# Node degrees by one-hot products: one-hot tables laid out with the tile number inside the class number

## The chip, the cores and the metric

The kernel runs on one core of a Trainium2 chip. The metric is the device time of one execution in microseconds (us). Five engines work side by side: PE (TensorE, matrix products; PEld is its weight load), DVE (VectorE), ACT (ScalarE), POOL (GpSimd) and SP (SyncE, which issues most plain transfers). They meet through semaphores.

## The reference, cut to what matters

A graph of 6250 nodes with 128 features and 106250 edges (each drawn edge in both directions, and a loop on each node) goes through two layers. The first is a graph convolution, the second an attention over edges. What the change touches is the number of edges that end in each node:

```python
deg = jax.ops.segment_sum(ones, dst, num_segments=n)
dinv = jnp.where(deg > 0, jax.lax.rsqrt(deg), 0.0)
norm = dinv[src] * dinv[dst]
msg = xw[src] * norm[:, None]
out = jax.ops.segment_sum(msg, dst, num_segments=n) + b
```

The kernel scales the normalised features of each node by `dinv` first, so no row of the first layer can be gathered before all degrees are known.

## The kernel before, in words

The edges lie as 832 tiles (`ET`) of 128: partition p of tile t holds one edge. The first block of the program does the following.

- **Degrees.** An end node `dst` is split in a low part (`dlo`, 0 to 63) and a high part (`dhi`, 0 to 97), both of 16-bit floats, `[128, 832]`. For each tile a one-hot table of 64 classes for the low part and one of 98 for the high part are made, and PE multiplies them: the product, 64x98, summed over all tiles in one PSUM bank, is the table of counts. The work goes in rounds of two slots, a slot holding 16 tiles (`BATCH`), 26 rounds in all (`ROUNDS`), 52 slots. `round` (line 340) makes DVE fill a slot with two comparisons, 1568 elements per partition for the high part (line 345) and 1024 for the low (line 346). PE takes the slot with 16 matmuls (line 794). With two slots DVE may fill one while PE reads the other: DVE waits on `hot_used` before it fills a slot again, PE waits on `hot_lanes`.
- **What lies between the rounds.** The first two calls of `round` stand before and in a loop of 13 iterations (line 350), each with one round and four `bn_stats` (line 355) on four tiles of the features `x`, which wait for the transfer of `x`. After the loop DVE does two reductions and a few small steps that wait for ACT and POOL (lines 358 to 366). Then 12 more rounds run with nothing between them (line 367).
- **The layout before.** A slot is `[16 tiles, classes]`, so a matmul reads 64 or 98 elements of 16 bits that lie one behind another. The comparison reads the row of class numbers `iota_h` again for each tile, and the tile's values from `dhi_twice` and `dlo_twice`, copies of `dhi` and `dlo` in which each value stands twice (lines 327 and 329), since the two comparisons run in inner pairs.
- **After the degrees.** One small step of DVE, two matmuls, a square root on ACT and a reciprocal give `dinv`. DVE scales all rows, `h`, in four parts (line 384), SP stores each to the table `y_tab` in HBM, and POOL waits for all four stores before its first gather (line 275). From there to the end of the block POOL issues 832 indirect gathers, one per tile of edges. A later block gathers rows of the second layer in 864 more.
- **ACT beside it.** It runs a warm-up, then counts by bucket (`sum_below`, line 680) from the moment when `buckets_ready` is given, which DVE does after the copies and four steps on `src`.

The order on each engine is as the code is written; no scheduler moves anything. All tables of one-hots and the `twice` copies lie in `sort_hi`, a buffer that is used for something else later on. `sort_v1` is idle during the whole degree stage.

Of the kernel before, what the change touches and what calls it, by code (L numbers as in the profile page):

```python
# [4 lines left out]
F32, F16, BF16 = mybir.dt.float32, mybir.dt.float16, mybir.dt.bfloat16  # L5
I32, U16 = mybir.dt.int32, mybir.dt.uint16
ALU = mybir.AluOpType
ACT = mybir.ActivationFunctionType
# [3 lines left out]
P = 128  # L12
# [13 lines left out]
ET = BODIES * BODY  # L26
EG = BODIES * GROUPS
LAST_TILE, LAST_FILL = EDGES // P, EDGES % P
HALF, HALVES = P // 2, 2 * NB
BATCH, SLOTS = 16, 2  # L30
# [27 lines left out]
def build(nc, x_in, src_in, dst_in, dst_rows_in, w0_in, b0_in, wqkv_in, bqkv_in, gamma_in, beta_in,  # L58
# [6 lines left out]
    def sem(name):  # L65
        return ctx.enter_context(nc.semaphore(name))
# [7 lines left out]
    with ctx:  # L74
# [58 lines left out]
        with ExitStack() as c1, nc.Block() as block:  # L133
            def sb1(name, shape, dt=F32):
                return c1.enter_context(nc.sbuf_tensor(name, shape, dt))

            def ps1(name, shape):
                return c1.enter_context(nc.psum_tensor(name, shape, F32))


            iota_h = sb1("iota_h", [P, 512], F16)
# [24 lines left out]
            dlo = sb1("dlo", [P, SORT_T], F16)  # L166
            dhi = sb1("dhi", [P, SORT_T], F16)
# [10 lines left out]
            tiles = sb1("tiles", [P, 2, NB])  # L178
# [11 lines left out]
            sort_v1 = sb1("sort_v1", [P, 2, SORTS, P], F16)  # L190
# [1 line left out]
            sort_hi = sb1("sort_hi", [P, 2, SORTS, max(WIDTH)], F16)  # L192

            flat_hi = sort_hi[:, :, :, :].rearrange("p a b c -> p (a b c)").bitcast(BF16)
            ohlo = flat_hi[:, 0:SLOTS * HALF * BATCH].rearrange("p (a b c) -> p a b c", a=SLOTS, b=BATCH)
            ohhi = flat_hi[:, SLOTS * HALF * BATCH:SLOTS * (HALF + HALVES) * BATCH].rearrange("p (a b c) -> p a b c", a=SLOTS, b=BATCH)
            twice_at = SLOTS * (HALF + HALVES) * BATCH
            dlo_twice, dhi_twice = (flat_hi[:, twice_at + n * 2 * ET:twice_at + (n + 1) * 2 * ET].bitcast(F16)
                                    .rearrange("p (t two) -> p t two", two=2) for n in range(2))
            tile_f, first_f = (flat_hi[:, n * 2 * SORT_T:(n + 1) * 2 * SORT_T].bitcast(F32) for n in range(2))  # L200
            b0_high = dhi[:, 0:2 * D].bitcast(BF16).rearrange("p (a b) -> p a b", a=2)
            b0_low = dlo[:, 0:4 * D].bitcast(F32).rearrange("p (a b) -> p a b", a=2)
# [4 lines left out]
            lane_i = tmp_i[:, 0:1]  # L207

            ps_sum = [ps1(f"ps_sum{k}", [P, 512]) for k in range(2)]
            ps_iota = ps1("ps_iota", [P, 512])  # L210
            ps_more = ps1("ps_more", [P, 512])
            ps_sort = [[ps1(f"ps_sort{n}{m}", [P, 512]) for m in range(2)] for n in range(2)]
            ps_row, ps_cnt, ps_deg = ps_sort[0][0], ps_sort[0][1], ps_sort[1][0]
            ps_run = ps_sort[1]

# [1 line left out]
            iota_ready, const_ready = sem("iota_ready"), sem("const_ready")  # L217
            ends_ready, rows_done = sem("ends_ready"), sem("rows_done")
            stats_done = sem("stats_done")
            shifted_ready, tiles_deg_done = sem("shifted_ready"), sem("tiles_deg_done")  # L220
            lanes_ready, deg_done = sem("lanes_ready"), sem("deg_done")
            hot_lanes, hot_used = sem("hot_lanes"), sem("hot_used")
            var_ready, std_done, norm_ready, h_done = sem("var_ready"), sem("std_done"), sem("norm_ready"), sem("h_done")
# [19 lines left out]
            def _(sp):  # L243
# [16 lines left out]
                sp.wait_ge(y_stored, 16 * Y_PARTS)  # L260


            in_twos = lambda t: t.rearrange("p k (c two) -> p k c two", two=2)
            every = lambda width: iota_h[:, 0:width].rearrange("p (c two) -> p c two", two=2)\
                .unsqueeze(1).to_broadcast([P, BATCH, width // 2, 2])
            each = lambda twice, tiles, width: twice[:, tiles, :].unsqueeze(2).to_broadcast([P, BATCH, width // 2, 2])

            @block.gpsimd
            def _(pool):
# [19 lines left out]
            def _(v):  # L289
# [34 lines left out]
                past = slice(LAST_TILE, LAST_TILE + 1)  # L324
                then(nc.vector.tensor_scalar(dlo[:, past], dlo[:, past], bad[:, :], None, ALU.add))
                nc.vector.memset(dlo[:, LAST_TILE + 1:ET], 2048.0).then_inc(lanes_ready, 1)
                nc.vector.tensor_copy(dhi_twice[:, :, :], dhi[:, 0:ET].unsqueeze(2).to_broadcast([P, ET, 2]))
                v.wait_ge(lanes_ready, 1)
                nc.vector.tensor_copy(dlo_twice[:, :, :], dlo[:, 0:ET].unsqueeze(2).to_broadcast([P, ET, 2])).then_inc(lanes_ready, 1)


                v.wait_ge(in_src, 16)
# [7 lines left out]
                def round(i):  # L340
                    for n in range(SLOTS):

                        v.wait_ge(hot_used, i * SLOTS + n + 1)
                        tiles = ds((i * SLOTS + n) * BATCH, BATCH)
                        nc.vector.tensor_tensor(in_twos(ohhi[:, n, :, :]), every(HALVES), each(dhi_twice, tiles, HALVES), ALU.is_equal)
                        nc.vector.tensor_tensor(in_twos(ohlo[:, n, :, :]), every(HALF), each(dlo_twice, tiles, HALF), ALU.is_equal).then_inc(hot_lanes, 1)

                v.wait_ge(lanes_ready, 2)
                round(0)
                with v.Fori(0, NODE_QUADS) as i:  # L350
                    round(i + 1)
                    v.wait_ge(in_x, 16)
                    part = ds(i * QUAD, QUAD)
                    for k in range(QUAD):
                        nc.vector.bn_stats(stats[:, part, :][:, k:k + 1, :], x[:, part, :][:, k:k + 1, :]).then_inc(stats_done, 1)
# [11 lines left out]
                with v.Fori(NODE_QUADS + 1, ROUNDS) as i:  # L367
                    round(i)
# [307 lines left out]
            def _(act):  # L676

                def sum_below(begin, end):

                    with act.Fori(begin, end) as i:  # L680
                        for n, unused in enumerate((tmp_f, away)):
                            b = i * 2 + n

                            act.wait_ge(below_ready, b + 1)
                            for part in range(2):
                                last = nc.scalar.activation(unused[:, PARTS[part]], sbk[:, PARTS[part]], ACT.Relu, bias=iota[:, ds(b + 1, 1)],
                                                            scale=-1.0, accum_out=below[:, part, ds(b + 2, 1)])
                            last.then_inc(below_ready, 1)
# [2 lines left out]
                act.wait_ge(const_ready, 1)  # L691

                nc.scalar.activation(warm[:, :], ones[:, 0:1], ACT.Sqrt)
                act.wait_ge(buckets_ready, 1)
                sum_below(0, EARLY)
                act.wait_ge(var_ready, 1)
# [3 lines left out]
                with act.Fori(0, NODE_QUADS) as n:  # L700
                    for k in range(QUAD):
                        j = n * QUAD + k
                        last = nc.scalar.activation(h[:, ds(j, 1), :], x[:, ds(j, 1), :], ACT.Relu, bias=nbias[:, ds(j, 1)],
                                                    scale=rstd[:, ds(j, 1)])
# [72 lines left out]
            def _(pe):  # L777
# [12 lines left out]
                with pe.Fori(0, ROUNDS) as i:  # L790
                    for n in range(SLOTS):
                        pe.wait_ge(hot_lanes, (i + 1) * SLOTS + n + 1)
                        for k in range(BATCH):
                            last = nc.tensor.matmul(ps_deg[0:HALF, 0:HALVES], ohlo[:, n, k, :], ohhi[:, n, k, :], start=False, stop=False)
                        last.then_inc(hot_used, 1)
                nc.tensor.matmul(ps_deg[0:HALF, 0:HALVES], zeros_h[:, 0:HALF], zeros_h[:, 0:HALVES], start=False, stop=True).then_inc(deg_done, 1)

# [2 lines left out]
                for n in range(2):  # L800
                    last = nc.tensor.matmul(ps_deg[:, HALVES:HALVES + NB], shifted[0:HALF, (1 - n) * HALF:(1 - n) * HALF + P],
                                            by_half[0:HALF, :].rearrange("p (j b) -> p j b", b=2)[:, :, n], start=n == 0, stop=n == 1)
# [3 lines left out]
                for n in range(2):  # L806
                    last = nc.tensor.matmul(ps_row[0:1, n * EG:(n + 1) * EG], ends_f[:, n:n + 1], ident[0:EG, 0:EG], start=True, stop=True)
# [42 lines left out]
                for part in range(2):  # L850
# [16 lines left out]
                    if part > 0:  # L867

                        pe.wait_ge(bk_ready, 2)
                        for g in range(ST // P):  # L870
                            c = g * P
                            last = nc.tensor.matmul(ps_sort[0][c // 512][0:1, c % 512:c % 512 + P], bk[:, 0, g:g + 1], ident[:, :],
                                                    start=True, stop=True)
# [3 lines left out]
                    for m in range(2):  # L877
                        last = nc.tensor.matmul(ps_sort[part][m][:, 0:w], zeros_h[:, 0:P], zeros_h[:, 0:w], start=False, stop=True)
# [4 lines left out]
        with ExitStack() as c3, nc.Block() as block:  # L883
            def sb3(name, shape, dt=F32):
                return c3.enter_context(nc.sbuf_tensor(name, shape, dt))
# [5 lines left out]
            a = sb3("a", [P, 2, QUAD, D])  # L891
# [674 lines left out]
```

## Time and profile before

| | us |
|---|---|
| median of 3 runs | 2404.34 |
| lowest and highest | 2402.21, 2406.58 |
| the profiled execution | 2402.21 |
| its span in the trace | 2400.4 |

```profile
PE 1599.1 (67%) x9620; PEld 1274.6 (53%) x9621; DVE 1776.6 (74%) x4811; ACT 1075.2 (45%) x3047; POOL 1683.3 (70%) x1772
```

The row gives the busy time of each engine in us, its share of the span and how many instructions it ran. No engine is busy all the time. Which one sets the pace changes from stage to stage, so the rows further down are taken by stage: start and duration of single instructions, what ended the idle time before them (in square brackets), and busy times in stretches.

### The profile page before, as it was taken

The page shows a single profiled execution, that of the slowest core. Times are in us where ns is not written, and L with a number is a line of the kernel's source. Part 1 is how long each engine was busy: PE and PEld are TensorE (multiplying, and loading weights), DVE is VectorE, ACT ScalarE, POOL GpSimd, SP SyncE. Part 2 cuts the span into 40 slices and gives each one's busy share as a digit, 9 for nine tenths or more (in the row PEclk, how much of TensorE's full clock was granted, in tenths as well). Part 3 has the DMA queues.
Part 4 walks back from the last instruction along what each step waited for, and adds up shares of the span by engine and source line. Part 5 has one row for each costly group of instructions (what it writes and reads, how often), then busy time and mean ns, then how long its engine had stood idle before and what let it go on. Part 6 is the DMA issues. An engine that isn't in the chain of part 4 may idle for free. (4 is left out here: it accounts for less than half of the span.)

```text
span 2400.4 us, 39858 instructions
## 1 busy us (share of the span) xinstructions
PE 1599.1 (67%) x9620; PEld 1274.6 (53%) x9621; DVE 1776.6 (74%) x4811; ACT 1075.2 (45%) x3047; POOL 1683.3 (70%) x1772
## 2 busy tenths in 40 slices
PE   5444439777878877777876665766766766676660
PEld 4334436555555555555655565655655655565560
DVE  9989999677767876667676666666666666666668
ACT  8734449777676877776751111111111111111113
POOL 0077777777777777777457777777777777777765
PEclk8857659888988888988989889789789788978875
DMA  2112211112121221121133333333333333333341
GB/s 89 54 51 53 53 52 52 52 51 52 52 52 52 53 52 52 52 52 52 26 127 104 104 104 104 104 105 105 104 104 104 105 104 102 103 105 104 104 98 54
DMA packets 84223, 186.36 MB, mean 78 GB/s; under 512 B 27773, under 2 KB 41213, under 8 KB 84069
## 3 DMA queue, kind: packets, MB, share of 16 engines
q0 software_dynamic: 68096, 167.88, 25.4%
q1 hardware_dynamic: 16101, 18.19, 2.3%
q8 instruction: 9, 0.15, 0.0%
q14 instruction: 17, 0.14, 0.0%
HBM read 173.11 MB, written 12.85 MB: 77 GB/s over the span
## 5 line engine op out<-in xcount | busy, mean ns | idle before, releaser
L1181 POOL DMA_INDIRECT kv_rows<-kv_tab,kv_idx x864 | 824.7, 955 | 274.5 <-issue 202.5
L283 POOL DMA_INDIRECT rows<-y_tab,idx x832 | 793.1, 953 | 308.6 <-issue 308.3
L1338 PE MATMUL ps_q<-q,hotT 128*128 x1744 | 312.5, 334 | 203.7 <-ACT hotT L1300 203.6
L763 ACT ACTIVATE sort_v<-sort_t,staged,minus 128x128 f16<-128x128 f16 x914 | 360.7, 480 | 114.8 <-PE ps_sort L860 113.1
L1338 PEld LDWEIGHTS ps_q<-q,hotT 128*128 128x128 f32 x1744 | 263.6, 231 | 257.9 <-issue 257.9
L602 DVE TENSOR_SCALAR sort_v<-iota_h,staged 128x128 f16<-128x128 f16 x748 | 250.7, 335 | 164.6 <-PE ps_sort L860 164.2
L860 PE MATMUL ps_sort<-sort_hi,sort_v 128*128 128x496 f16 x1662 | 366.2, 378 | 0.6 <-ACT sort_v L763 0.6
L818 PE MATMUL ps_sum<-rows,hot 128*128 128x128 f32 x1664 | 260.4, 322 | 145.3 <-DMA rows<-y_tab,idx 104.5
L1204 DVE TENSOR_TENSOR prod<-ps_q,kv_rows 128x512 f32<-128x512 f32 x216 | 149.4, 692 | 270.0 <-DMA kv_rows<-kv_tab,kv_idx 270.0
L1316 ACT ACTIVATE msg<-attc 128x32 f32<-128x32 f32 x216 | 49.5, 229 | 659.6 <-DVE attc L1216 659.6
L818 PEld LDWEIGHTS ps_sum<-rows,hot 128*128 128x128 f32 x1664 | 250.5, 237 | 159.8 <-issue 89.2
L1348 PE MATMUL ps_m<-msg,kv_hot 128*128 128x136 f32 x1728 | 306.8, 334 | 0.0
L755 ACT ACTIVATE sort_t<-iota_h,minus 128x128 f16<-128x128 f16 x831 | 250.9, 387 | 101.8 <-DVE minus L594 101.8
L1348 PEld LDWEIGHTS ps_m<-msg,kv_hot 128*128 128x128 f32 x1728 | 287.4, 244 | 0.0
L604 DVE TENSOR_SCALAR sort_hi<-iota_h,staged 128x496 f16<-128x496 f16 x831 | 286.1, 352 | 0.0
L1329 PE MATMUL ps_hT<-ident,kv_hot 128*128 128x128 f32 x876 | 157.7, 308 | 174.1 <-DVE kv_hot L1195 173.4
L1239 DVE TENSOR_TENSOR acc<-acc,ps_m 128x136 f32 x864 | 249.7, 289 | 21.9 <-PE ps_m L1348 20.3
L860 PEld LDWEIGHTS ps_sort<-sort_hi,sort_v 128*128 128x128 f16 x1662 | 165.5, 100 | 178.9 <-issue 11.3
L818 PE MATMUL ps_more<-rows,more_hot 128*128 128x128 f32 x768 | 143.0, 363 | 172.3 <-DMA rows<-y_tab,idx 105.3
L1300 ACT ACTIVATE hotT<-ps_hT 128x512 f32<-128x512 f32 x218 | 130.2, 597 | 236.6 <-PE ps_hT L1329 236.6
L818 PEld LDWEIGHTS ps_more<-rows,more_hot 128*128 128x128 f32 x768 | 133.2, 269 | 186.2 <-issue 185.7
L1329 PEld LDWEIGHTS ps_hT<-ident,kv_hot 128*128 128x128 f32 x876 | 111.1, 158 | 211.2 <-DVE kv_hot L1195 210.3
(236 smaller groups left out, 1864.1 us busy)
## 6 DMA issues: line engine op xcount, KB each, us to landing
kv_rows<-kv_tab,kv_idx POOLq DMA_INDIRECT x864, 2.7
rows<-y_tab,idx POOLq DMA_INDIRECT x832, 2.5
kv_tab<-kv SPq DMA_DIRECT2D x12, 512.0 KB, 2.9
x<-x_in SPq DMA_DIRECT2D x1, 3328.0 KB, 14.1
out<-h SPq DMA_DIRECT2D x12, 256.0 KB, 2.0
y_tab<-h SPq DMA_DIRECT2D x1, 1088.0 KB, 6.6
y_tab<-h SPq DMA_DIRECT2D x1, 960.0 KB, 5.7
y_tab<-h SPq DMA_DIRECT2D x1, 704.0 KB, 4.1
```

What stands on the lines that cost most here:

```text
L283: pool.indirect_dma_start(out=rows[:, k * SPAN + n, :], out_offset=None, in_=y_tab, in_offset=bass.IndirectOffsetOnAxis(ap=idx[:, k, n:n + ...
L602: nc.vector.tensor_scalar(sort_v2[:, k % 2, m, :], iota_h[:, 0:P], staged[:, LO, c:c + 1], staged[:, V2, c:c + 1], ALU.is_equal, ALU.mult)
L604: last = nc.vector.tensor_scalar(sort_hi[:, k % 2, m, 0:WIDTH[part]], iota_h[:, 0:WIDTH[part]], staged[:, HI, c:c + 1], None, ALU.is_equal)
L755: last = nc.scalar.activation(sort_t[:, k % 2, m, :], iota_h[:, 0:P], ACT.Abs, bias=minus[:, LO, k * SORTS + m:k * SORTS + m + 1])
L763: last = nc.scalar.activation(to[:, k % 2, m, :], sort_t[:, k % 2, m, :], ACT.Relu, bias=staged[:, v, c:c + 1], scale=minus[:, v, c:c + 1])
L818: last = nc.tensor.matmul(ps[:, 0:D], hots[:, n, :], rows[:, k * SPAN + n, :], start=n == 0, stop=n == SPAN - 1)
L860: last = nc.tensor.matmul(ps[:, 0:w], values[:, k % 2, m, :], sort_hi[:, k % 2, m, 0:w], start=False, stop=False)
L1181: pool.indirect_dma_start(out=rows[:, u, k, :], out_offset=None, in_=kv_tab, in_offset=bass.IndirectOffsetOnAxis(ap=idx[:, u, k:k + 1], ax ...
L1239: nc.vector.tensor_tensor(acc[:, ds(b, 1), :], acc[:, ds(b, 1), :], ps_m[u % 2][k // 2][:, k % 2:k % 2 + 1, 0:MSG], ALU.add).then_inc(tile ...
L1329: last = nc.tensor.transpose(ps_hT[u % 2][:, k, :], hot[:, u, k, :], ident[:, :])
L1338: last = nc.tensor.matmul(ps_q[u % 2][:, k, :], hotT[:, u % 2, k, :], q[:, ds(buckets[k], 1), :], start=True, stop=True)
L1348: last = nc.tensor.matmul(ps_m[u % 2][k // 2][:, k % 2, 0:MSG], hot[:, u, k, :], msg[:, u, k, :], start=True, stop=True)
```

## The change

The tables of a slot become `[classes, 16 tiles]`: the tile number runs fastest. The comparison now reads the values of 16 tiles straight from `dhi` and `dlo`, repeated for each class, and the class numbers from a new table `iota_b` in which each of 128 numbers stands 16 times. ACT makes it once, in `sort_v1`, between its warm-up and `sum_below`; DVE waits for it before the first round. The two `twice` copies go. PE reads a tile's table as every 16th element, a step of 32 bytes, for the weights (64 elements) and for the moving side (98). The bank of `ps_iota` moves from the third to the last place of the PSUM tensors, which shifts the banks of `ps_more` and `ps_sort` down by one.

```diff
-            ohlo = flat_hi[:, 0:SLOTS * HALF * BATCH].rearrange("p (a b c) -> p a b c", a=SLOTS, b=BATCH)
-            ohhi = flat_hi[:, SLOTS * HALF * BATCH:SLOTS * (HALF + HALVES) * BATCH].rearrange("p (a b c) -> p a b c", a=SLOTS, b=BATCH)
-            twice_at = SLOTS * (HALF + HALVES) * BATCH
-            dlo_twice, dhi_twice = (flat_hi[:, twice_at + n * 2 * ET:twice_at + (n + 1) * 2 * ET].bitcast(F16)
-                                    .rearrange("p (t two) -> p t two", two=2) for n in range(2))
+            ohlo = flat_hi[:, 0:SLOTS * HALF * BATCH].rearrange("p (a b c) -> p a b c", a=SLOTS, b=HALF)
+            ohhi = flat_hi[:, SLOTS * HALF * BATCH:SLOTS * (HALF + HALVES) * BATCH].rearrange("p (a b c) -> p a b c", a=SLOTS, b=HALVES)
+            iota_b = sort_v1[:, :, :, :].rearrange("p a b c -> p (a b c)")[:, 0:P * BATCH].rearrange("p (a b) -> p a b", a=P)
...
-            ps_iota = ps1("ps_iota", [P, 512])
             ps_more = ps1("ps_more", [P, 512])
             ps_sort = [[ps1(f"ps_sort{n}{m}", [P, 512]) for m in range(2)] for n in range(2)]
+            ps_iota = ps1("ps_iota", [P, 512])
...
-            in_twos = lambda t: t.rearrange("p k (c two) -> p k c two", two=2)
-            every = lambda width: iota_h[:, 0:width].rearrange("p (c two) -> p c two", two=2)\
-                .unsqueeze(1).to_broadcast([P, BATCH, width // 2, 2])
-            each = lambda twice, tiles, width: twice[:, tiles, :].unsqueeze(2).to_broadcast([P, BATCH, width // 2, 2])
+            every = lambda width: iota_b[:, 0:width, :]
+            each = lambda columns, tiles, width: columns[:, tiles].unsqueeze(1).to_broadcast([P, width, BATCH])
...
-                nc.vector.tensor_copy(dhi_twice[:, :, :], dhi[:, 0:ET].unsqueeze(2).to_broadcast([P, ET, 2]))
-                v.wait_ge(lanes_ready, 1)
-                nc.vector.tensor_copy(dlo_twice[:, :, :], dlo[:, 0:ET].unsqueeze(2).to_broadcast([P, ET, 2])).then_inc(lanes_ready, 1)
...
-                        nc.vector.tensor_tensor(in_twos(ohhi[:, n, :, :]), every(HALVES), each(dhi_twice, tiles, HALVES), ALU.is_equal)
-                        nc.vector.tensor_tensor(in_twos(ohlo[:, n, :, :]), every(HALF), each(dlo_twice, tiles, HALF), ALU.is_equal).then_inc(hot_lanes, 1)
-
-                v.wait_ge(lanes_ready, 2)
+                        nc.vector.tensor_tensor(ohhi[:, n, :, :], every(HALVES), each(dhi, tiles, HALVES), ALU.is_equal)
+                        nc.vector.tensor_tensor(ohlo[:, n, :, :], every(HALF), each(dlo, tiles, HALF), ALU.is_equal).then_inc(hot_lanes, 1)
+
+                v.wait_ge(lanes_ready, 1)
+                v.wait_ge(iota_b_ready, 1)
...
                 nc.scalar.activation(warm[:, :], ones[:, 0:1], ACT.Sqrt)
+                nc.scalar.activation(iota_b, iota_h[:, 0:P].unsqueeze(2).to_broadcast([P, P, BATCH]), ACT.Copy).then_inc(iota_b_ready, 1)
...
-                            last = nc.tensor.matmul(ps_deg[0:HALF, 0:HALVES], ohlo[:, n, k, :], ohhi[:, n, k, :], start=False, stop=False)
+                            last = nc.tensor.matmul(ps_deg[0:HALF, 0:HALVES], ohlo[:, n, :, k], ohhi[:, n, :, k], start=False, stop=False)
```

DVE before the change, from the last step on `dlo` to the first slot (all one-hot tables and both copies are parts of `sort_hi`):

```order
L326 MEMSET dlo 128x1 [waits dve]
L327 COPY sort_hi<-dhi 128x1664
L329 COPY sort_hi<-dlo 128x1664 [waits lanes_ready]
L333 MEMSET src_c 128x32 [waits in_src]
L334 TENSOR_SCALAR tmp_i<-src_c 128x832
L335 CAST sbk<-tmp_i 128x832 [waits dve]
L336 TENSOR_SCALAR sbk<-sbk,bad 128x1 [waits dve]
L337 MEMSET sbk 128x9 [waits dve]
L345 TENSOR_TENSOR sort_hi<-iota_h,sort_hi 128x1568 [waits hot_used,lanes_ready]
L346 TENSOR_TENSOR sort_hi<-iota_h,sort_hi 128x1024
```

The same place after the change (`sort_v` is the buffer that holds `iota_b`):

```order
L322 MEMSET dlo 128x1 [waits dve]
L326 MEMSET src_c 128x32 [waits in_src]
L327 TENSOR_SCALAR tmp_i<-src_c 128x832
L328 CAST sbk<-tmp_i 128x832 [waits dve]
L329 TENSOR_SCALAR sbk<-sbk,bad 128x1 [waits dve]
L330 MEMSET sbk 128x9 [waits dve]
L338 TENSOR_TENSOR sort_hi<-sort_v,dhi 128x1568 [waits hot_used,iota_b_ready,lanes_ready]
L339 TENSOR_TENSOR sort_hi<-sort_v,dlo 128x1024
```

The two copies are gone, everything behind them moves up, and the first comparison has one more thing to wait for. ACT at the start of the program after the change:

```order
L687 ACTIVATE warm<-ones 128x1 [waits const_ready]
L688 ACTIVATE sort_v<-iota_h 128x2048
L674 UNCONDITIONAL_BRANCH [waits buckets_ready]
L674 ISA
L680 ISA [waits below_ready]
L680 ACTIVATE cols,below<-sbk,iota 128x440
```

The step at line 688 is new; before, the wait on `buckets_ready` stood right behind the warm-up. PE's instructions are the same in number and order.

## Rows read from the trace of the kernel before

**Rows 1.** Stretches: start:end, us, POOL busy, granted PE clock, DMA share, GB/s.

```profile
121.00:1167.00 1046.00, 792.75 (x832) 0.83 0.20 52
1248.00:2335.00 1087.00, 824.15 (x864) 0.84 0.36 104
```

**Rows 2.** Waits of POOL: us in total, times, longest.

```profile
POOL rows L283 <- issue: 308.3, 831, 55.4
```

**Rows 3.** Timeline, 97 to 150: start, duration, instruction, idle before and releaser.

```profile
103.08 0.91 PE L794 MATMUL ps_sort<-sort_hi 128*64 128x98 bf16 x16 [0.58 <-DVE sort_hi L346]
...
105.12 0.21 ACT L708 ACTIVATE deg<-ps_sort 128x49 f32<-128x49 f32 x1 [8.12 <-PE ps_sort L801]
...
120.82 1.17 POOL L283 DMA_INDIRECT rows<-y_tab,idx  x1 [55.36 <-issue]
```

**Rows 4.** Timeline of DVE at the start of the degree stage.

```profile
7.16 1.02 DVE L327 COPY sort_hi<-dhi 128x1664 f16<-128x1664 f16 x1
...
9.07 0.09 DVE L333 MEMSET src_c<- 128x32 int32 x1
...
10.62 0.98 DVE L345 TENSOR_TENSOR sort_hi<-iota_h,sort_hi 128x1568 bf16<-128x1568 f16 x1
...
16.93 0.86 DVE L355 BATCH_NORM_STATS2 stats<-x  x4
```

**Rows 5.** Transfers: KB each, us from issue to landing; timeline of the issue of `x`.

```profile
x<-x_in SPq DMA_DIRECT2D x1, 3328.0 KB, 14.1
...
src_c<-src_in SPq DMA_DIRECT2D x1, 416.0 KB, 3.8
...
1.66 0.42 SPq L246 DMA_DIRECT2D x<-x_in  x1
```

**Rows 6.** Timeline of ACT: the warm-up, and a copy of 2560 elements per partition.

```profile
4.39 0.20 ACT L693 ACTIVATE warm<-ones 128x1 f32<-128x1 f32 x1 [2.31 <-DVE ident L315]
...
113.21 2.34 ACT L713 ACTIVATE acc<-h 128x2560 f32<-128x2560 f32 x1 [0.93 <-DVE h L384]
```

**Rows 7.** Timeline, second loop, at the high clock.

```profile
76.17 0.97 DVE L345 TENSOR_TENSOR sort_hi<-iota_h,sort_hi 128x1568 bf16<-128x1568 f16 x1
...
77.66 0.97 DVE L345 TENSOR_TENSOR sort_hi<-iota_h,sort_hi 128x1568 bf16<-128x1568 f16 x1
77.79 0.77 PEld L794 LDWEIGHTS ps_sort<-sort_hi 128*64 128x64 bf16 x16 [0.72 <-DVE sort_hi L346]
```

**Rows 8.** Timeline, second loop, at the low clock.

```profile
68.25 1.33 PEld L794 LDWEIGHTS ps_sort<-sort_hi 128*64 128x64 bf16 x16 [5.33 <-DVE sort_hi L346]
...
69.94 0.97 DVE L345 TENSOR_TENSOR sort_hi<-iota_h,sort_hi 128x1568 bf16<-128x1568 f16 x1 [0.25 <-PE ps_sort L794]
```

**Rows 9.** Timeline of DVE, first loop: the four `bn_stats` and the next slot.

```profile
28.16 0.87 DVE L355 BATCH_NORM_STATS2 stats<-x  x4
28.94 0.96 DVE L345 TENSOR_TENSOR sort_hi<-iota_h,sort_hi 128x1568 bf16<-128x1568 f16 x1
```

**Rows 10.** Stretches, line 794 alone: PE busy, PEld busy, granted clock, DMA share, GB/s.

```profile
26.00:42.00 16.00, 12.21 (x131) 10.79 (x132) 0.50 0.00 0
...
68.00:72.00 4.00, 3.43 (x38) 3.09 (x39) 0.50 0.00 0
74.00:103.00 29.00, 17.27 (x304) 14.62 (x304) 1.00 0.00 0
```

**Rows 11.** Timeline of DVE between the two loops.

```profile
62.65 1.22 DVE L358 TENSOR_REDUCE ends_i<-rows 104x1 int32<-104x1024 int32 x1
...
66.62 0.98 DVE L345 TENSOR_TENSOR sort_hi<-iota_h,sort_hi 128x1568 bf16<-128x1568 f16 x1
```

**Rows 12.** Timeline of PE: eight 32-bit matmuls of 128 columns, and that stretch's clock.

```profile
1300.21 1.15 PE L1338 MATMUL ps_q<-q,hotT 128*128 x8 [1.27 <-ACT hotT L1300]
1300.20:1301.40 1.20, 1.19 (x10) 1.19 (x11) 0.91 (x3) 0.00 (x0) 0.94 (x1) 1.00 0.36 109
```

**Rows 13.** Groups: a comparison with 32-bit operands; busy us, mean ns, idle before.

```profile
L450 DVE TENSOR_TENSOR hot<-ps_iota,rel 128x1024 f32<-128x1024 f32 x13 | 15.8, 1217 | 2.3 <-issue 2.3
```

More of the change, by code:

```diff
@@ L219, in build @@
             stats_done = sem("stats_done")
-            shifted_ready, tiles_deg_done = sem("shifted_ready"), sem("tiles_deg_done")
+            iota_b_ready, shifted_ready, tiles_deg_done = sem("iota_b_ready"), sem("shifted_ready"), sem("tiles_deg_done")
             lanes_ready, deg_done = sem("lanes_ready"), sem("deg_done")
```

## The prediction, made before the changed kernel ran

> **What bounds the kernel now.** I read the stages first. From 121 to 1167 us POOL issues the 832 gathers of the first layer and from 1248 to 2335 the 864 of the second [rows 1]: 792.75 us of busy time in 1046, which with a gap of 0.3 us before each gather is one gather per 1.25 us without a break. So everything behind the first gather is a fixed train, and it starts when the first gather may. The waits of POOL say how long that is: one idle time of 55.4 us stands before line 283, by far its longest [rows 2]. Then the timeline at that place [rows 3]: the last group of 16 degree matmuls starts at 103.08, ACT's square root at 105.12 had waited 8.12 us for PE, then DVE scales `h`, the stores follow, and POOL starts at 120.82. Nothing there has slack. The time of the kernel moves one for one with the end of the degree stage, and what the change does before about 104 us is the whole of its effect. All my sums are the shift of that end.
>
> Within the stage, DVE is the pace. At the high clock a slot costs it 77.66 - 76.17 = 1.49 us; PE starts a group 77.79 - 76.17 = 1.62 us after DVE began the slot, and feeds it in 0.77 us, 48 ns per matmul [rows 7]. PE has half its time left. At the low clock the group takes 1.33 us, 83 ns per matmul, which is one column per clock at 1.2 GHz (98 / 1.2 = 82 ns); and DVE got the slot back only 69.94 - 68.25 = 1.69 us after the group began, and had waited 0.25 us [rows 8]. So there the loop over two slots, 1.62 + 1.69 = 3.31 us, just exceeds DVE's own 2.98. That is the margin that this prediction turns on. In the first loop `bn_stats` adds 28.94 - 28.16 = 0.78 us [rows 9] and a round takes 3.76, more than 3.31.
>
> **The change part by part.**
>
> Copies. They go: from 7.16 to 9.07, 1.91 us off DVE [rows 4], and DVE begins the first slot at 8.71 instead of 10.62. `x` is issued at 1.66 and lands 14.1 us later, at 15.8; `src`, issued ahead of it, takes 3.8 and is there by 5.5, so it doesn't hold the step that moves up [rows 5]. The first `bn_stats`, at 16.93 before [rows 4], would come at 15.02 and wait 0.8 us for it. So the removal is worth 1.1 us where nothing else is late, and 1.9 where something else already is.
>
> `iota_b` on ACT. A copy of 2560 elements takes 2.34 us there [rows 6], so 2048 take about 1.9; it starts after the warm-up, at 4.6, and ends at 6.5, ahead of the 8.71 at which DVE wants it. Behind it on ACT stands `sum_below`, which waits for `buckets_ready` until 8.7 or later. Price 0; it would have to take twice as long before it cost anything. Its input repeats each element 16 times, which no row here shows; a price of nothing to 2 us more stays covered.
>
> The comparisons on DVE. Same element counts and types, all 16 bits wide with step 1 inside. A slot of 2592 elements in 1.49 us is 1.35 us at two elements per clock of 0.96 GHz and 0.14 of fixed cost. There is nothing to gain but the fixed part, 52 x 0.14 = 7 us at most; the far end is the comparison with 32-bit operands, 1.22 us for 1024 elements [rows 13], where the slot would take 3.1 us. Nothing in the new pattern speaks for either; price 0. The bank of `ps_iota`: 0, since the stage doesn't read it and no later wait hangs on DVE's comparisons.
>
> PE's reads. This is the disputed term. Number and order of the matmuls stay, but each column is now a separate 32-byte step, for weights and moving side. No row shows a 16-bit read of that kind. From below: 48 ns per matmul at the high clock, as now [rows 7]. From above: the 32-bit matmuls of the second layer, where PE takes in twice the bytes per column: eight of 128 columns in 1.15 us at a granted clock of 1.00 [rows 12]. Less the last one's 0.275 us (from there one end to the next) that is 125 ns each, 0.98 ns per column, or 96 ns for 98 columns. I take two clocks per column, 82 ns at 2.4 GHz and 163 at 1.2, near that row. The Trainium skill points the same way (SBUF — State Buffer, the note on cachelines under "Door 1: The DMA port swizzle"; also Advanced Engine Details and Errata, "SBUF Cachelines"): lines are 16 bytes, a reader needs about two hits on each to hide the memory's latency, and 16-bit data can be stepped by up to 8 elements for free. The step here is 16 elements. The pages give no size for the penalty; by their rule the sum is that of my forecast or of the slow rivals, and no run shown so far tests it.
>
> The sum with two clocks per column, clock levels as in the trace before (low until about 6 us after the first group, low again for about 4.5 us after the pause between the loops, high from 74 on [rows 10]):
> - copies: -1.9.
> - start, low clock: groups take 16 x 0.163 = 2.61 us. The first runs 10.33 to 12.94 and frees its slot 0.38 later, at 13.32; DVE was ready at 11.69: 1.63 late. The second ends at 15.55, frees at 15.93; DVE was ready at 14.81: 1.12 late. Less the 0.3 it waited before: +2.5. That also hides the wait for `x`.
> - rest of the first loop at the high clock: 1.62 + 1.69 = 3.31 is under 3.76: 0.
> - pause (62.65 to 66.62 [rows 11]): unchanged. After it again two low-clock groups, 1.63 + 0.74 late, less 0.3 that it waited before: +2.1.
> - eleven further rounds of the second loop: 3.31 against 2.98, 11 x 0.33 = +3.6.
> - last group, 1.31 against 0.77: +0.5.
> Sum +6.8 us on the profiled execution's 2402.2, which lies 2.1 under the median of 2404.3; against the median 2411. The form's own range: with less tail after a group about +5; with 0.98 ns per column a round of the second loop is 3.54 us and the sum near +10; and where PE stays at the low level in the first loop for as long as it did before (it stood at 0.50 from 26 to 42 although 76% busy [rows 10]), 24 us of rounds at 2 x 2.61 = 5.22 instead of 3.76 add 24 / 5.22 x 1.46 = 7, +14 in all. So 2409 to 2418.
>
> **The rivals.**
>
> A, the step costs PE nothing. Then only the copies count: -1.1, 2403.2. For it: PE's columns might be fetched ahead, and PE idles half of each slot, 17.27 us busy in 29 [rows 10], so even 30 ns more per matmul would hide. Against it: the 32-bit rows show that PE's column rate does depend on what it must fetch. It decides wherever the group stays below 2.98 - 1.62 = 1.36 us including its tail. This is the side on which the kernel isn't slower.
>
> B, a fixed time per line and not per clock: 82 ns at either level. At the low clock nothing changes, at the high clock the second loop behaves as in rows 8: -1.1 + 11 x 0.33 + 0.5 = +3.0, 2407.3.
>
> C, PE becomes the bound for good: two clocks per column at a level that stays low, or four at the high one, 163 ns either way. For it: the stretch 26 to 42, low at 76% busy [rows 10]. Against it: fewer idle gaps than ever before, and both loops did rise. All groups then run back to back: DVE gets to its last slot of the first loop at 10.33 + 26 x 2.61 + 0.38 = 78.6, is through `bn_stats` and the pause at 84.8, PE starts at 86.4 and ends 24 x 2.61 later at 149.1, where it was 103.85: +45, 2449. A price between, 120 ns at the high clock (1.92 us per group), gives 24 x 0.43 = 10 in the second loop and some 5 elsewhere: +16.
>
> D, DVE gets faster, since the class numbers now stream through and the inner run is 16 and not 2: at the most the fixed 0.14 per slot goes, 52 x 0.14 + 1.1 = -8, 2396. For it speaks only that the fixed part exists; against it that consecutive instructions already overlap.
>
> **How the numbers follow.** Forecast 32%, A 29%, B 12%, C with what lies between 22%, D 5%. Of this kernel 0.2%, 4.8 us, is about what a measurement tells from no change. Slower by more: the forecast but for its lowest end (0.28), C (0.22), the top of B (0.02): 0.52. Within: A (0.27), most of B (0.10), the low end of the forecast (0.04): 0.41. Faster: D and a stray of A: 0.07. The range starts a little under A, at 2401.5, which leaves out D, and ends at C, 2450: about one in ten is left out.
>
> **What would show it.** Right: in the second loop line 789 takes about 82 ns per matmul at a granted clock of 1.00 and line 338 waits some 0.3 us in every round for PE; the first POOL gather starts near 127.6. The copies' step: line 326 at 7.2 and line 338 at 8.7. A is right if the groups still take 0.77 us and line 349 first waits for the transfer of `x`. C is right if PE is busy without a gap from 10 to beyond 120. I am wrong in kind if lines 338 and 339 change their durations, or if the interval from the last group to the first gather, 17.7 us before, moves.

## The result, and the profile after

The changed kernel takes 2463.01 us in the median of 4 runs, against 2404.24 for the kernel before: 58.8 us more, a ratio of 1.0246 with a 95% interval of 1.0233 to 1.026. I had forecast slower, with 2411 as the time and 2450 as the upper end of the range. The way was right and the size was wrong by a factor of more than eight. Executions of one kernel scatter: the kernel before took between 2402.21 and 2406.58 us.

Timeline of DVE, start of the degree stage after the change (the copies are gone, compare [rows 4]):

```profile
7.20 0.09 DVE L326 MEMSET src_c<- 128x32 int32 x1
...
8.78 0.98 DVE L338 TENSOR_TENSOR sort_hi<-sort_v,dhi 128x1568 bf16<-128x1568 f16 x1
...
13.69 0.98 DVE L338 TENSOR_TENSOR sort_hi<-sort_v,dhi 128x1568 bf16<-128x1568 f16 x1 [1.85 <-PE ps_sort L789]
...
16.56 0.98 DVE L338 TENSOR_TENSOR sort_hi<-sort_v,dhi 128x1568 bf16<-128x1568 f16 x1 [1.30 <-PE ps_sort L789]
...
18.06 0.87 DVE L349 BATCH_NORM_STATS2 stats<-x  x4
```

The first slot starts 1.84 us earlier than before. From the third slot on DVE waits for PE, and goes on doing so. Timeline of DVE in the second loop, which answers to [rows 7]:

```profile
114.00 0.97 DVE L338 TENSOR_TENSOR sort_hi<-sort_v,dhi 128x1568 bf16<-128x1568 f16 x1 [1.30 <-PE ps_sort L789]
...
116.88 0.97 DVE L338 TENSOR_TENSOR sort_hi<-sort_v,dhi 128x1568 bf16<-128x1568 f16 x1 [1.30 <-PE ps_sort L789]
```

A slot now takes 116.88 - 114.00 = 2.88 us where it took 1.49. That is 180 ns for each of the 16 matmuls of a slot, where it was 48 at the high and 83 at the low clock. The groups of the whole degree stage (8 to 163 us; busy us, mean ns, idle before; since matmuls overlap, 832 of them in 150.1 us of busy time are 180 ns each, and the mean of 360 is the length of one from its start to its end):

```profile
L789 PE MATMUL ps_sort<-sort_hi 128*64 128x98 bf16 x832 | 150.1, 360 | 7.7 <-DVE sort_hi L339 7.7
L789 PEld LDWEIGHTS ps_sort<-sort_hi 128*64 128x64 bf16 x832 | 149.4, 196 | 8.2 <-DVE sort_hi L339 8.2
L338 DVE TENSOR_TENSOR sort_hi<-sort_v,dhi 128x1568 bf16<-128x1568 f16 x52 | 50.7, 975 | 54.2 <-PE ps_sort L789 54.1
```

PE idles 7.7 us, of which 5.5 stand before the first slot and the rest in the pause between the loops, and DVE has 54.1 us of waits for it: the bound has moved from DVE to PE. DVE's own instructions kept their duration (975 ns on average, 971 before). Timeline at the end of the stage, which answers to [rows 3]:

```profile
162.58 0.26 PE L791 MATMUL ps_sort<-zeros_h 128*64 128x98 f16 x1
...
164.37 0.21 ACT L703 ACTIVATE deg<-ps_sort 128x49 f32<-128x49 f32 x1 [42.12 <-PE ps_sort L796]
...
180.08 1.17 POOL L279 DMA_INDIRECT rows<-y_tab,idx  x1 [89.39 <-issue]
```

ACT's square root and the first gather both come 59.3 us later than before (105.12 and 120.82). Behind it nothing absorbs the delay. Stretches of POOL as in [rows 1], moved by 59 and 60 us (the second layer's gathers begin at 1306.72, so one of the 864 falls ahead of the stretch):

```profile
180.00:1226.00 1046.00, 792.75 (x832) 0.85 0.20 52
1308.00:2395.00 1087.00, 823.57 (x863) 0.84 0.37 104
```

The same 832 gathers in the same 1046 us, and the last gather of the second layer starts at 2393.24 where it started at 2334.26, 59.0 us later. So the delay of the degree stage is carried to the end, and it makes up the 58.8 us within the scatter of executions. The two profiled executions themselves are 61.4 us apart in span; the 2.4 us more lie behind the last gather and are within that scatter too.

### The profile page after: what moved, and what is told of

Same layout as the page of the kernel before. It is cut to its first block and busy times, and to the rows that moved or that the text cites. A ratio compares the mean times of both kernels' runs of the same rounds, so it can differ in the third digit from the quotient of the medians.

```text
span 2461.8 us, 39857 instructions
## 1 busy us (share of the span) xinstructions
PE 1685.7 (68%) x9620; PEld 1370.5 (56%) x9621; DVE 1777.6 (72%) x4809; ACT 1077.3 (44%) x3048; POOL 1683.0 (68%) x1772
## 5 line engine op out<-in xcount | busy, mean ns | idle before, releaser
L813 PE MATMUL ps_sum<-rows,hot 128*128 128x128 f32 x1664 | 249.1, 313 | 146.6 <-DMA rows<-y_tab,idx 102.9
L813 PEld LDWEIGHTS ps_sum<-rows,hot 128*128 128x128 f32 x1664 | 239.4, 228 | 160.4 <-issue 87.7
```

Source lines behind the costliest of these rows:

```text
L813: last = nc.tensor.matmul(ps[:, 0:D], hots[:, n, :], rows[:, k * SPAN + n, :], start=n == 0, stop=n == SPAN - 1)
```

## The experiments

For most experiments there is one execution, beside one of the kernel before (2405.74 us) or the median of 21 (2403.75, from 2401.09 to 2406.35); only `WIDE = 2` and the two runs built on it have 11. So a difference of a few microseconds between single totals tells nothing by itself, and the readings below go by the time per matmul in the traces.

Theory 1 at the start: both of PE's inputs go through one path, 64 + 98 = 162 separate reads in 180 ns. Theory 2: the moving side alone sets the price.

**Only the moving side stepped.** The changed kernel, with the low part's table and its pair copy back in the old layout:

```diff
-ohlo = flat_hi[...].rearrange("p (a b c) -> p a b c", a=SLOTS, b=HALF)
+ohlo = flat_hi[...].rearrange("p (a b c) -> p a b c", a=SLOTS, b=BATCH)
-matmul(ps_deg[0:HALF, 0:HALVES], ohlo[:, n, :, k], ohhi[:, n, :, k], ...)
+matmul(ps_deg[0:HALF, 0:HALVES], ohlo[:, n, k, :], ohhi[:, n, :, k], ...)
```

> Only the moving side (98 columns) is read with the 32-byte step; the weights (64) are contiguous as before. Theory 1 (weights and moving side go through one read path, 64 + 98 = 162 separate reads in the 180 ns that a matmul took, 1.11 ns each): 98 x 1.11 = 109 ns per matmul, a group in 1.74 us, total about 2415. Theory 2 (the moving side alone sets the price, 180 / 98 = 1.83 ns per column, the weight load stays hidden): still 180 ns per matmul, total 2462 or so.

Measured: 2466.03 us beside 2405.74 for the kernel before. Its group of the degree stage:

```profile
L797 PE MATMUL ps_sort<-sort_hi 128*64 128x98 bf16 x832 | 148.8, 358 | 8.8 <-DVE sort_hi L347 8.8
```

148.8 us for 832 matmuls is 179 ns each. The weights, now contiguous, change nothing. Theory 1 is out.

**Only the weights stepped.** The mirror image: `ohhi` and its pair copy in the old layout, `ohlo` with the step.

> Only the weights (64) are read with the 32-byte step; the moving side (98) is contiguous. Theory 1: 64 x 1.11 = 71 ns of reads for weights, hidden beside the 82 ns that 98 columns take at the low clock if the two overlap: total 2403 to 2407. If the two reads add up, 71 + 82 = 153 ns and about 2443. Theory 2: 48 or 82 ns per matmul as before the change, total 2403.

Measured: 2425.32 us, 19.6 more than before. Timeline of DVE:

```profile
98.74 0.97 DVE L346 TENSOR_TENSOR sort_hi<-iota_h,sort_hi 128x1568 bf16<-128x1568 f16 x1 [0.42 <-PE ps_sort L797]
...
102.70 0.97 DVE L346 TENSOR_TENSOR sort_hi<-iota_h,sort_hi 128x1568 bf16<-128x1568 f16 x1 [0.42 <-PE ps_sort L797]
```

Two slots in 3.96 us, 124 ns per matmul, or 1.9 ns for each of the 64 weights. None of the totals that I expected (2403 to 2407, 2443, 2403) was met. Theory 2 as I had put it is wrong too: the weights have the same price. The two sides run side by side and the dearer one counts: 98 elements in 180 ns hide 64 in 124.

**Half the columns.** The changed kernel with a moving side of 49 columns. Its output lacks part of the degrees.

```diff
-matmul(ps_deg[0:HALF, 0:HALVES], ohlo[:, n, :, k], ohhi[:, n, :, k], ...)
+matmul(ps_deg[0:HALF, 0:NB], ohlo[:, n, :, k], ohhi[:, n, 0:NB, k], ...)
```

> The changed kernel with only the first 49 of 98 columns of the moving side multiplied (the counts of the upper half of the high classes are left out; DVE fills all of them still). Theory L with the two sides side by side: the 64 weights now set the price, 64 x 1.83 to 1.92 = 117 to 123 ns, about 2425. If the two sides took turns on one path: (64 + 49) x 1.11 = 125 ns, the same; but then the run with only the moving side stepped should have been cheaper than it was. If only the moving side counts: 49 x 1.83 = 90 ns, about 2410.

Measured: 2419.61 us. Timeline of DVE:

```profile
94.25 0.98 DVE L338 TENSOR_TENSOR sort_hi<-sort_v,dhi 128x1568 bf16<-128x1568 f16 x1 [0.42 <-PE ps_sort L789]
...
102.09 0.98 DVE L338 TENSOR_TENSOR sort_hi<-sort_v,dhi 128x1568 bf16<-128x1568 f16 x1 [0.39 <-PE ps_sort L789]
```

Four slots in 7.84 us, 122.5 ns per matmul, the figure of the run with only the weights stepped. With 49 columns the 64 weights are the longer side. The total came 5 us below what I expected, the time per matmul within it; I had taken the total from the run with only the weights stepped, and what parts the two single totals is open.

**The size of the step.** The slot as groups of `WIDE` tiles, `[16/WIDE, classes, WIDE]`. DVE's comparisons keep their counts; `WIDE = 16` is the changed kernel.

```diff
-ohhi = flat_hi[...].rearrange("p (a b c) -> p a b c", a=SLOTS, b=HALVES)
+ohhi = flat_hi[...].rearrange("p (a g b c) -> p a g b c", a=SLOTS, g=BATCH // WIDE, b=HALVES)
-matmul(..., ohlo[:, n, :, k], ohhi[:, n, :, k], ...)
+matmul(..., ohlo[:, n, k // WIDE, :, k % WIDE], ohhi[:, n, k // WIDE, :, k % WIDE], ...)
```

`WIDE = 8`, a step of 16 bytes:

> The slot is laid out as 2 x [classes, 8 tiles], so PE's step is 16 bytes for both sides; DVE's work is that of the changed kernel. If a read costs by the 16-byte line that it opens (lines: each element still lies in a line of its own), the price stays 180 ns per matmul and the total 2463. If the price follows the step above a bound that 8 elements just meet, or follows the bytes spanned (half of them now), it falls: to 82 ns or below, total 2403 to 2406, or to about 90 to 110 ns, total about 2412.

Measured: 2463.57 us, beside 2463.01 for the changed kernel. Timeline of DVE:

```profile
115.19 0.98 DVE L340 TENSOR_TENSOR sort_hi<-sort_v,dhi 128x1568 bf16<-128x1568 f16 x1 [1.25 <-PE ps_sort L791]
...
118.02 0.97 DVE L340 TENSOR_TENSOR sort_hi<-sort_v,dhi 128x1568 bf16<-128x1568 f16 x1 [1.25 <-PE ps_sort L791]
```

2.83 us per slot, 177 ns per matmul: half the step, nearly the same price.

`WIDE = 4`, 8 bytes:

> The slot is laid out as 4 x [classes, 4 tiles]: PE's step is 8 bytes, two elements per 16 bytes. By lines: no price beyond the contiguous 48 ns at the high and 82 ns at the low clock, so only the removed copies count: total 2403, about 1 us under the kernel before. If any step other than 1 costs (the rival), 100 to 180 ns per matmul and 2415 to 2463.

Measured: 2412.14 us, 6.4 more than before; POOL's first gather comes at 125.95 instead of 120.82, 5.1 later. Weight loads of two groups each, first at a granted clock of 0.50, then at 1.00, and the stretches of line 791 that say so:

```profile
26.98 2.92 PEld L791 LDWEIGHTS ps_sort<-sort_hi 128*64 128x64 bf16 x32 [0.83 <-DVE sort_hi L341]
...
95.67 2.94 PEld L791 LDWEIGHTS ps_sort<-sort_hi 128*64 128x64 bf16 x32 [0.48 <-DVE sort_hi L341]
```

```profile
20.00:40.00 20.00, 16.87 (x177) 15.48 (x176) 0.50 0.00 0
...
76.00:96.00 20.00, 18.38 (x190) 16.52 (x189) 1.00 0.00 0
```

2.92 / 32 = 91 ns at the low and 2.94 / 32 = 92 ns at the high clock: half of 180, and independent of the clock. My expectation (no price beyond the contiguous one) was wrong; at the high clock the contiguous 48 ns have become 92, at the low clock the contiguous 83 have become 91.

`WIDE = 2`, 4 bytes:

> The slot is laid out as 8 x [classes, 2 tiles]: PE's step is 4 bytes, four elements per 16 bytes; no twice copies. Theory L (1.83 ns for each 16-byte piece that a side opens): 98 / 4 x 1.83 = 45 ns per matmul, under the 48 that it costs anyway, so PE is as in the kernel before and only the copies count: 1.1 us less than before, 0.9995 of it. Theory S (a price for the mere step, falling with it: 180, 177, 92 ns at 32, 16 and 8 bytes): about 60 to 70 ns per matmul, DVE waits for PE at times, 0 to 3 us more than before.

Measured: 2403.89 us in 11 runs against 2403.75, ratio 1.0, interval 0.9991 to 1.0009. That is too wide to tell the 1.1 us of gain that theory L gave from none. Timeline of PE's weight loads at the high clock:

```profile
90.64 0.78 PEld L791 LDWEIGHTS ps_sort<-sort_hi 128*64 128x64 bf16 x16 [0.71 <-DVE sort_hi L341]
```

0.78 us per group, as contiguous [rows 7]; theory S wanted 60 to 70 ns per matmul and is out. This run keeps everything of the change but the wide step: the copies are gone, ACT makes `iota_b`, the bank has moved. Its total is that of the kernel before, so the 58.8 us are the price of PE's step.

So a step of 32, 16, 8 and 4 bytes costs 180, 177, 92 and 49 ns per matmul, the last two at the high clock. This is what one reader per side would give that needs about 1.8 ns for every new piece of 16 bytes: 98 pieces, 98, 49, and 25, where the last is under the 48 ns that the columns take anyway. The prices are measured; the pieces are the reading that fits them, since no run moved the elements within a piece at the same step. The Trainium skill's note on cachelines (SBUF — State Buffer, "Door 1: The DMA port swizzle") names 16 bytes as the line, and the equal price at 16 and 32 bytes agrees. It also holds a step of 8 elements for free; here that step cost 177 ns against 48, and even the step of 4 elements, two per line, cost 92. The measurement decides.

**The bank of `ps_iota` back in its old place**, added to `WIDE = 2`:

```diff
+ps_iota = ps1("ps_iota", [P, 512])
 ps_more = ps1("ps_more", [P, 512])
 ps_sort = [...]
-ps_iota = ps1("ps_iota", [P, 512])
```

> As the run with step 4, with ps_iota in its old bank. If the bank is worth nothing (every theory so far): the same time as that run within 0.1%. If the bank has a part in it, the two differ by more than 1 us, in the scans and comparisons behind the degree stage.

Measured: 2404.49 us, ratio to the kernel before 1.0002 (0.9993 to 1.0011); 0.6 us from the run without it, inside both intervals. The bank has no part in the total that can be measured.

**PE brought to the high clock first.**

```diff
+with pe.Fori(0, 48) as i:
+    nc.tensor.matmul(ps_more[:, :], iota_h[:, 0:P], iota_h[:, :], start=True, stop=True)
 with pe.Fori(0, ROUNDS) as i:
```

> The changed kernel with 48 contiguous matmuls of 512 columns ahead of the degree loop, into a bank that is overwritten later; they occupy PE from about 5 to 18 us and should bring it to the high clock. If the price of the step is a fixed time (1.83 ns per column, theory L): the first strided groups take 180 ns per matmul although PE is at the high clock, and the total is that of the changed kernel plus the 8 us of delay, about 2471. If the price is in PE clocks (2.2 per column, rival): 90 ns per matmul for as long as the clock stays up, and the total falls by what lasts, down to about 2415 to 2430 if it stays up.

Measured: 2475.42 us. Line 792 in the two stretches, and the slots behind them:

```profile
23.30:26.30 3.00, 3.00 (x17) 3.00 (x18) 1.00 0.00 0
30.00:60.00 30.00, 30.00 (x168) 30.00 (x167) 0.50 0.00 0
```

```profile
49.55 0.98 DVE L339 TENSOR_TENSOR sort_hi<-sort_v,dhi 128x1568 bf16<-128x1568 f16 x1 [0.52 <-PE ps_sort L792]
...
52.43 0.98 DVE L339 TENSOR_TENSOR sort_hi<-sort_v,dhi 128x1568 bf16<-128x1568 f16 x1 [1.30 <-PE ps_sort L792]
```

At 1.00, 17 matmuls fall in 3.00 us, 176 ns each but for what the edges of the stretch cut off, and from one start to the next it is 180; at 0.50 the slot takes 2.88 us, 180 ns each. That the high level was real shows in the warm-up: its matmuls of 512 columns start 427 ns apart up to 9.1 us, and right behind it some start 216 ns apart. The price is a time and not a count of PE clocks. The warm-up itself lasted to 23.2 us instead of 18, since from 10.4 us on its matmuls start 0.38 us apart, which makes the total 12 us more than the changed kernel's and not 8.

**`x` ahead of the weights**, added to `WIDE = 2`:

```diff
+sp.wait_ge(in_x, 16)
 sp.dma_start(dst_rows, dst_rows_in).then_inc(in_rows, 16)
```

> The run with step 4 with one thing more: the transfers of the edge rows and of the weights are issued after x has landed, not beside it. Theory: in the run with step 4 the 1.9 us of the removed copies were lost again to the wait for x before the first bn_stats (0.73 to 1.90 us, and 0.6 us of unhidden issue behind it); with x there earlier (by about a sixth of its 14 us) that wait is gone and the first gather of POOL starts 1.7 to 2.0 us earlier than in the kernel before, at about 119; the total is about 0.9992 of it, which the timing may not tell from 1. Rival: the wait is not what eats the gain, and the first gather stays at 120 or later.

The wait that it is about, in the run with `WIDE = 2`, and the same place with `x` ahead:

```profile
15.87 0.49 DVE L351 BATCH_NORM_STATS2 stats<-x  x2 [0.73 <-DMA x<-x_in]
16.63 0.49 DVE L351 BATCH_NORM_STATS2 stats<-x  x2 [0.27 <-issue]
17.47 0.98 DVE L340 TENSOR_TENSOR sort_hi<-sort_v,dhi 128x1568 bf16<-128x1568 f16 x1 [0.35 <-issue]
```

```profile
15.05 0.48 DVE L352 BATCH_NORM_STATS2 stats<-x  x2
15.76 0.48 DVE L352 BATCH_NORM_STATS2 stats<-x  x2 [0.22 <-issue]
16.59 0.97 DVE L341 TENSOR_TENSOR sort_hi<-sort_v,dhi 128x1568 bf16<-128x1568 f16 x1 [0.35 <-issue]
...
119.77 1.17 POOL L282 DMA_INDIRECT rows<-y_tab,idx  x1 [55.39 <-issue]
```

The wait for `x` is gone and POOL's first gather comes at 119.77, 1.05 us earlier than before; I had expected 1.7 to 2.0. What stays are the gaps of 0.22 and 0.35 us in the first pass of the loop, put down to issue. One trace each is thin ground for 1.05 us, for the landing of `x` moves by more from trace to trace. Where `WIDE = 2` alone waited 0.73 us for it and had its first gather at 120.31, the run with the bank in its old place waited 1.90 us and had it at 121.79:

```profile
17.05 0.48 DVE L351 BATCH_NORM_STATS2 stats<-x  x2 [1.90 <-DMA x<-x_in]
```

Measured with `x` ahead: 2405.56 us against 2406.28, ratio 0.9996 (0.9987 to 1.0005). The wait is shown to go; a gain in time is not shown. No version here is measurably faster than the kernel before.

## Why the prediction was wrong

- **The frame held.** Everything behind the first gather is a fixed train: gather and total moved by 59.3 and 58.8 us. The interval from the last group to the first gather, which I had named as a sign of being wrong in kind, did move: from the group's start by the 2.1 us that the group itself takes longer, and from its end by some 0.5 us, which go with the clock (see below).
- **Copies, `iota_b`, comparisons, bank: right.** 1.84 us forward against 1.91; the table was ready before DVE wanted it; the comparisons kept their time; the bank is worth nothing that can be measured. That `x` would be waited for without them is shown by the run with `WIDE = 2`.
- **The step that failed** is "PE's reads. ... I take two clocks per column, 82 ns at 2.4 GHz and 163 at 1.2", with 96 ns from the 32-bit matmuls as the bound from above. It is one term, mis-sized: 180 ns at either clock. Two mistakes are in it. First, that row is no bound from above for a stepped read: the 32-bit operands are contiguous and share a 16-byte piece between four columns, while here every column opens its own. It bounded another mechanism. (The row is also weaker than I read it: the loop behind it issues four matmuls, and the trace has two records for each.) Second, I tied the price to PE's clock, which put most of the forecast at the high level's 82 ns.
- **The clock level was wrong as well, at little cost.** The forecast had PE at the high level from about 6 us after the first group. The rows of the changed kernel do say 1.00 for the whole stage, but its trace holds no record of the level before 205 us, and a stretch without one reads as 1.00. The small 32-bit matmuls right behind the stage tell: 0.61 us in the kernel before, 1.06 in the changed one, and 1.06 in the warmed run, whose trace has the low level on record there. The kernel before, at 1.00:

```profile
104.47 0.61 PE L801 MATMUL ps_sort<-by_half,shifted 64*128 64x49 f32 x4 [0.44 <-DVE by_half L374]
```

The changed kernel, and then the warmed run with the granted clock of that stretch (0.50, the third figure from the end):

```profile
163.28 1.06 PE L796 MATMUL ps_sort<-by_half,shifted 64*128 64x49 f32 x4 [0.44 <-DVE by_half L368]
```

```profile
176.12 1.06 PE L799 MATMUL ps_sort<-by_half,shifted 64*128 64x49 f32 x4 [0.44 <-DVE by_half L369]
175.50:177.20 1.70, 1.26 (x7) 1.01 (x6) 0.68 (x3) 0.00 (x0) 0.00 (x0) 0.50 0.00 0
```

So PE was at the low level when the stage ended, and nothing shows that it had been higher before. With a price that is a time this cost the stage nothing, and the steps behind it the 0.5 us.

- **With the right price the working gives the result.** Rival C's sum with 2.88 us per group instead of 2.61: the last slot of the first loop at 10.4 + 26 x 2.88 + 0.4 = 85.7, through `bn_stats` and the pause at 91.9 (the trace has 91.84), PE at 93.5, end 24 x 2.88 later at 162.6, where the trace has 162.4. Less 103.85: +58.7.
- **Rival C** had the mechanism, PE the bound for good, and 163 ns; its sign, PE busy without a gap from 10 us to beyond 120, came true but for one gap of 2.3 us in the pause. At 22% and with its time as the end of the range it was under-weighted and still too small. Rival B had the other half, a fixed time at either clock, with 82 ns.

The range failed since its upper end was worked out from rows of contiguous reads, while the changed access was of a kind that no row showed. That the forecast got the way right is partly luck: 3.6 of its 6.8 us came from a loop at the high clock, 3.31 us against 2.98 per round, which never ran.

## What to carry to other kernels

Keep the 16-bit elements that PE reads one after another close together: a step of 16 or 32 bytes made a small matmul of 64 weights and 98 columns take 177 to 180 ns, against 48 contiguous at the high clock and 83 at the low one, and the weights pay like the moving side. If another engine's layout asks for interleaving, interleave as little as it needs: with two elements DVE's comparisons kept their duration (972 ns on average, 971 before) and PE paid nothing. And when a trace shows no case of an access, a row with a like number of bytes is no upper bound for it. Here PE had half its time left at the high clock (0.77 of 1.49 us per slot) and the price still went past it.

## What the runs showed of the hardware that I had not expected

- The price of a stepped read doesn't follow PE's clock: 91 and 92 ns at 0.50 and 1.00 for the 8-byte step, 180 at either for the 32-byte one.
- A PE that the trace shows busy without a gap was granted the low level: 30.00 us busy of 30.00 at 0.50 in the warmed run. The level had risen at 9.2 us, under the contiguous matmuls, and fell at 26.3, after PE had gone over to the stepped ones at 23.3. It cost nothing there, since the price was not in clocks; why the level fell with PE busy is left open.
